# Issuing the first samples from SP and ACT, holding back weights and the second unit's samples, and reordering rows and copies at the start of a routed MLP kernel

## The reference

```
s0  = relu(x @ swi[0]) @ swo[0]            # shared unit, all samples
s1  = relu(x @ swi[1]) @ swo[1]
eo  = relu(x @ wi[label]) @ wo[label]      # the sample's own expert, 256 -> 1024 -> 256
gate_in = concat(eo[:, 0], s0[:, 0], s1[:, 0])          # row 0 of each sample only
w   = softmax(relu(gate_in @ g1) @ g2)                   # 3 numbers per sample
x   = x + eo * w[0] + s0 * w[1] + s1 * w[2]
x   = x + zX * lap_x(x) + zY * lap_y(x) + zR * x * (1 - x)   # second differences, reflected edges
```

## Time and profile before

| what | us |
|---|---|
| median of 3 runs | 1146.95 (1146.84 to 1147.79) |
| the profiled execution, its own time | 1147.54 |
| its span, first to last instruction | 1146.0 |
| PE busy | 1137.4 (99% of the span) |
| DVE busy | 676.5 (59%) |
| ACT busy | 455.7 (40%) |
| POOL busy | 79.8 (7%) |

### The profile page before, as it was taken

The page is one execution under the profiler, slowest core; times in us unless marked ns, Lnnn a source line. Parts: engine busy times, 40 slices in busy tenths (PEclk is TensorE's granted clock), DMA queues, the critical chain, the costliest instruction groups (busy, mean ns, idle before and its releaser), DMA issues.

```text
span 1146.0 us, 16857 instructions
## 1 busy us (share of the span) xinstructions
PE 1137.4 (99%) x6068; PEld 971.9 (85%) x6068; DVE 676.5 (59%) x1030; ACT 455.7 (40%) x808; POOL 79.8 (7%) x125
## 2 busy tenths in 40 slices
PE   8999999999999999999999999999999999999998
PEld 7888888888888888888888888888888888888888
DVE  4656666656666644556555655565465565556556
ACT  2555555555655532323323333333333233333323
POOL 3111211211211100000000000000000000000001
PEclk9999999999999999999999999999999999999999
DMA  8555556556565514023022121131230230321300
GB/s 277 158 162 170 171 169 204 180 152 195 179 191 150 163 34 117 16 68 78 17 73 46 47 76 27 57 84 23 62 83 16 69 81 13 74 45 49 75 29 24
DMA packets 111252, 111.83 MB, mean 98 GB/s; under 512 B 78441, under 2 KB 87234, under 8 KB 111170
## 3 DMA queue, kind: packets, MB, share of 16 engines
q1 hardware_dynamic: 96770, 59.71, 19.4%
q0 software_dynamic: 14016, 50.73, 14.8%
q10 hardware_dynamic: 384, 0.33, 0.1%
HBM read 89.40 MB, written 17.04 MB: 93 GB/s over the span
## 4 chain that ended last, share of the span: by engine, by line
PE 98%; DMA 1%; DVE 0%; issue 0%; ACTq 0%; ACT 0%; POOL 0%; DVEq 0%; POOLq 0%
PE acc L917 31%; PE hbank L890 16%; PE hbank L889 16%; PE hbank L891 16%; PE acc L918 16%; PE tbank L845 1%; DMA xs<-in_x 1%; PE acc L903 0%; PE hbank L870 0%; PE tbank L840 0%; PE acc L928 0%; PE acc L810 0%; PE acc L930 0%; PE acc L929 0%; PE tbank L853 0%
## 5 line engine op out<-in xcount | busy, mean ns | idle before, releaser
L582 DVE SCALAR_TENSOR_TENSOR hl<-hbank,hh 128x512 fp32r<-128x512 f32 (+2 forms) x440 | 275.7, 627 | 426.9 <-ACT hh L1022 426.3
L1022 ACT ACTIVATE hh<-hbank 128x512 fp32r<-128x512 f32 (+2 forms) x440 | 240.2, 546 | 587.9 <-PE hbank L891 584.9
L917 PE MATMUL acc<-swo,hh 128*128 128x512 f32 x992 | 359.3, 396 | 0.0
L918 PE MATMUL acc<-swo,hl 128*128 128x256 f32 x992 | 277.8, 280 | 0.0
L917 PEld LDWEIGHTS acc<-swo,hh 128*128 128x128 f32 x992 | 186.3, 188 | 43.7
L889 PE MATMUL hbank<-xh,swh 128*128 128x512 f32 (+1 forms) x528 | 205.3, 389 | 0.0
L890 PE MATMUL hbank<-xl,swh 128*128 128x512 f32 (+1 forms) x528 | 205.0, 388 | 0.0
L891 PE MATMUL hbank<-xh,swl 128*128 128x512 f32 (+1 forms) x528 | 202.1, 383 | 0.0
L917 PE MATMUL acc<-ewo,hh 128*128 128x512 f32 x528 | 194.6, 398 | 0.7 <-DVE rx L590 0.4
L918 PEld LDWEIGHTS acc<-swo,hl 128*128 128x128 f32 x992 | 187.1, 189 | 9.6
L918 PE MATMUL acc<-ewo,hl 128*128 128x256 f32 x528 | 148.0, 280 | 0.0
(11 more groups left out here) (194 smaller groups left out, 900.5 us busy)
## 6 DMA issues: line engine op xcount, KB each, us to landing
rw<-in_L_cond_wi POOLq DMA_DIRECT2D x44, 512.0 KB, 4.5
rw<-in_L_cond_wo POOLq DMA_DIRECT2D x44, 512.0 KB, 4.6
eo_scratch<-eo SPq DMA_DIRECT2D x128, 64.0 KB, 2.6
xs<-in_x SPq DMA_DIRECT2D x16, 512.0 KB, 4.3
rw<-in_x SPq DMA_DIRECT2D x256, 32.0 KB, 2.2
ei<-eo_scratch SPq DMA_DIRECT2D x16, 512.0 KB, 5.5
xs<-in_x SPq DMA_DIRECT2D x127, 64.0 KB, 3.5
out<-ot SPq DMA_DIRECT2D x15, 512.0 KB, 6.3
```

The lines of the kernel that those rows point to most:

```text
L582: e.scalar_tensor_tensor(h_slot(HL, g), bank[:, 0:w], 0.0, h_slot(HH, g).bitcast(F32), ALU.max, ALU.subtract).then_inc(h_lo, 1)
L917: e.matmul(acc[j][:, 0:2 * D], HH[:, g % NH, js], woc[:, c, :], start=(c == 0), stop=False)
L918: m = e.matmul(acc[j][:, D:2 * D], HL[:, g % NH, js], woc[:, c, 0:D], start=False, stop=last)
L1022: e.activation(h_slot(HH, g), hbank[g % HRING][:, 0:w], ACT.Relu).then_inc(h_hi, 1)
```

## The change

FIRST_BY gives samples 0 to 3 of unit 0 to ACT and 4 to 7 to SP; GpSimd loads none, and its semaphore `xp_in` goes. ACT issues at g == EARLY - 1 with EARLY = 6, so behind the relu of chunk 5, and the relus of chunks 6 and 7 are DVE's. GpSimd waits for `h_prod` 12 ahead of pieces 2, 1, 3 of unit 0, and SP waits for `h_prod` 12 ahead of unit 1's samples. The row of samples gets its own bank (`acc[2]`) and its own signal `row_prod`, so that DVE copies it behind one product of three; the float copy goes. PE puts the second products of chunks 2 and 3 ahead of the first products of chunks 4 and 5. Unit 0's transposes move from (2, 0) to (1, 7), still behind the first product of chunk 15 but now ahead of the second product of chunk 13, and unit 0's first product waits for each half of the low part by itself. DVE makes the low part of weight piece 0 at (1, 5) and not at (1, 7), and `evacuate(1)` stands ahead of `cut_low(2, 2)`.

```diff
@@ -28,10 +28,10 @@
-EARLY = 8
+EARLY = 6
 LAST_ORDER = (0, 2, 1, 3)
-FIRST_BY = {"ACT": (0, 1, 2), "SP": (3, 4, 5), "POOL": (6, 7)}
+FIRST_BY = {"ACT": (0, 1, 2, 3), "SP": (4, 5, 6, 7)}
@@ -81,7 +81,7 @@
-    if (n, c) == (2, 0):
+    if (n, c) == (1, 7):
         return [(1, 0), (1, 1)]
@@ -135,8 +135,8 @@
 SHARED_AT = (4, 6, 8, 10, 11, 13, 15, 17)
-FIRST_HIGH = {(1, 6): [(2, 0)], (2, 0): [(2, 2)], (2, 1): [(2, 1)], (2, 3): [(2, 3)]}
-FIRST_LOW = {(1, 7): [(2, 0)], (2, 0): [(2, 2)], (2, 2): [(2, 1)], (2, 4): [(2, 3)]}
+FIRST_HIGH = {(1, 4): [(2, 0)], (2, 0): [(2, 2)], (2, 1): [(2, 1)], (2, 3): [(2, 3)]}
+FIRST_LOW = {(1, 5): [(2, 0)], (2, 0): [(2, 2)], (2, 2): [(2, 1)], (2, 4): [(2, 3)]}
@@ -218,7 +218,7 @@
         msel = sb("msel", [128, NSLOT])
-        rowf = sb("rowf", [1, 2, NSLOT])
+        rowf = sb("rowf", [1, NSLOT])
         tab = sb("tab", [1, 3, NSLOT], I32)
@@ -264,6 +264,7 @@
         t_prod = sem("t_prod")
+        row_prod = sem("row_prod")
         t_hi = sem("t_hi")
@@ -271,7 +272,6 @@
         s_in = sem("s_in")
-        xp_in = sem("xp_in")
         w_hi = sem("w_hi")
@@ -380,8 +380,6 @@
             x_slot[tile % 2] += 16 * (slots_of(tile - 1)[1] if 1 <= tile <= NU else 1)
-            if tile == 1:
-                x_slot[1] -= 16 * len(FIRST_BY["POOL"])
             X_VAL[tile] = x_slot[tile % 2]
@@ -488,18 +486,17 @@
             def slot_table():
+                e.wait_ge(row_prod, 1)
+                e.tensor_copy(tab[:, 0, :], acc[2][0:1, 0:NSLOT]).then_inc(*V.up())
+                AT["samples"] = V.n
                 e.wait_ge(t_prod, T_AT["rows"])
-                e.tensor_copy(tab[:, 0, :], tbank[0:1, 0:NSLOT]).then_inc(*V.up())
-                AT["samples"] = V.n
-                e.tensor_copy(tab[:, 2, :], tbank[0:1, 2 * NSLOT:3 * NSLOT]).then_inc(*V.up())
+                e.tensor_copy(tab[:, 2, :], tbank[0:1, NSLOT:2 * NSLOT]).then_inc(*V.up())
                 AT["experts"] = V.n
-                e.tensor_copy(rowf[:].rearrange("p a n -> p (a n)"), tbank[0:1, 0:2 * NSLOT]).then_inc(t_free, 1)
+                e.wait_ge(consts, 7)
+                e.scalar_tensor_tensor(rowf[:], tbank[0:1, 0:NSLOT], 0.5, outdef[:],
+                                       ALU.is_lt, ALU.mult).then_inc(t_free, 1)
                 e.wait_ge(t_free, T_AT["rows"])
-                e.wait_ge(consts, 7)
-                e.scalar_tensor_tensor(rowf[:, 1, :], rowf[:, 1, :], 0.5, outdef[:],
-                                       ALU.is_lt, ALU.mult).then_inc(*V.up())
-                e.wait_ge(dve_seq, V.n)
-                e.tensor_tensor(tab[:, 1, :], rowf[:, 0, :], rowf[:, 1, :], ALU.add).then_inc(*V.up())
+                e.tensor_tensor(tab[:, 1, :], acc[2][0:1, 0:NSLOT], rowf[:], ALU.add).then_inc(*V.up())
                 AT["targets"] = V.n
@@ -715,6 +712,8 @@
                     slot_table()
+                if (n, c) == (1, NC - 1):
+                    hidden_low(g)
                 if g < G:
@@ -739,8 +738,9 @@
                 if (n, c) == (2, 0):
+                    evacuate(1)
                     cut_low(2, 2)
-                if g < G:
+                if g < G and (n, c) != (1, NC - 1):
                     hidden_low(g)
@@ -748,7 +748,7 @@
                     own_slot()
-                if g >= LAG and CHUNKS[g - LAG][1] == NC - 1 and CHUNKS[g - LAG][0] < NP - 2:
+                if g >= LAG and CHUNKS[g - LAG][1] == NC - 1 and CHUNKS[g - LAG][0] < NP - 2 and g - LAG != 2 * NC - 1:
                     evacuate(CHUNKS[g - LAG][0])
@@ -820,10 +820,9 @@
                 e.wait_ge(dve_seq, AT["msel"])
-                for a in range(2):
-                    e.matmul(tbank[0:1, a * NSLOT:(a + 1) * NSLOT], cols[:, a:a + 1], msel[:], start=True, stop=True)
-                e.matmul(tbank[0:1, 2 * NSLOT:3 * NSLOT], cols[:, 2:3], msel[:], start=True,
-                         stop=True).then_inc(t_prod, 1)
+                e.matmul(acc[2][0:1, 0:NSLOT], cols[:, 0:1], msel[:], start=True, stop=True).then_inc(row_prod, 1)
+                e.matmul(tbank[0:1, 0:NSLOT], cols[:, 1:2], msel[:], start=True, stop=True)
+                e.matmul(tbank[0:1, NSLOT:2 * NSLOT], cols[:, 2:3], msel[:], start=True, stop=True).then_inc(t_prod, 1)
@@ -831,7 +830,8 @@
                 if tile == 1:
-                    e.wait_ge(xp_in, 16 * len(FIRST_BY["POOL"]))
+                    e.wait_ge(dve_seq, AT["targets"])
                 if k is None:
@@ -874,7 +874,7 @@
                     to = bank[:, 0:w]
-                    if c == 0:
+                    if c == 0 and tile > 1:
                         e.wait_ge(t_free, T_AT[tile_last(tile)])
@@ -886,6 +886,8 @@
                 for k in range(2):
+                    if tile == 1 and c == 0:
+                        e.wait_ge(t_free, T_AT[tile, k])
                     e.matmul(to, wh[:, k, cs], xh[k], start=(k == 0), stop=False)
@@ -941,6 +943,8 @@
                     slot_rows()
+                if (n, c) == (1, NC - 1):
+                    first_product(g)
                 if g < G:
@@ -972,10 +976,14 @@
                     second_product(g - 1)
-                if g < G:
+                if g < G and (n, c) != (1, NC - 1):
                     first_product(g)
-                if g >= LAG and (n, c) not in ((2, 0), (2, 1)) and CHUNKS[g - LAG][0] < NP - 1:
+                if g >= LAG and (n, c) not in ((0, 4), (0, 5), (2, 0), (2, 1)) and CHUNKS[g - LAG][0] < NP - 1:
                     second_product(g - LAG)
+                if (n, c) == (0, 3):
+                    second_product(g - 1)
+                    second_product(g)
             for j, c in LAST_PRODUCTS:
@@ -1102,7 +1110,7 @@
                             cut_high(ws, p)
-                if (n, c) == (0, NC - 1):
+                if g == EARLY - 1:
                     first_samples()
@@ -1164,11 +1172,8 @@
             load_unit(0, (0,))
-            for b in FIRST_BY["POOL"]:
-                e.reg_load(reg, tab[0:1, 0, b:b + 1])
-                v = e.snap(reg, min_val=0, max_val=NS - 1)
-                e.dma_start(XS[1][b:128:8, :, :], x[bass.ds(v, 1), :, :].rearrange("a (p j) d -> (a p) j d", p=16)) \
-                    .then_inc(xp_in, 16)
+            e.wait_ge(h_prod, 12)
             load_unit(0, (2, 1, 3))
```

## The result

The changed kernel takes 1148.57 us, the median of 18 runs (1147.58 to 1150.47), against 1146.80 for the kernel before in its 18 (1145.17 to 1147.79). The ratio is 1.0017 with a 95% interval of 1.0010 to 1.0024. It is slower by 1.8 us, where I forecast no change at 1147.1 and a range that ended at 1148.2. The profiled execution took 1148.16 us, its span is 1146.6.

The account below looks back on a forecast made before the run. PE, busy 99% of the span, was taken as the bound. A 2.66 us gain on unit 0 would be spent waiting for unit 1's samples, net +0.1 us, so 1147.1 us, with a range of 1144.7 to 1148.2.

Parts of the forecast that it names:

- The wait for the gate-row copy: Ahead of unit 0's first second product: PE's 0.4 us wait for DVE goes, bringing the gain so far to 2.66 us.
- the one ahead of unit 0's first product: PE's 0.8 us wait there goes; the product starts at 24.55 in place of 26.54, 2.0 us gained.
- SP's first issue of unit 1: Behind the twelfth product (18.95): first sample issued at 19.4, eighth at 26.5, landing 6.4 us later at 32.9.
- The standstill in front of unit 1's transposes: PE wants these transposes at 30.2 but starts at 33.0, waiting for samples: idle for 2.8 us.
- the 2.66 us are gained and then spent: Ahead of unit 1's transposes: PE gains 2.66 us on unit 0, then loses it waiting for unit 1's samples.
- +0.1: Net effect at unit 1's transposes: they start at 33.0 against 32.9, so the time moves by +0.1 us.
- the third rival, "the clock falls, slower": Behind PE's idle stretch at unit 1's transposes, 5 us at the lower clock lose 2.5 us: 1149.6; chance 0.04.
- The first samples of unit 0: Ahead of unit 0's transposes: the last sample lands before 22.3, so they start at 22.35 without wait, 1.5 us earlier.

Follow-up runs that it names:

- the filled kernel: Changed kernel with ten extra matmuls, results overwritten, on PE ahead of its wait for unit 1's samples: 1147.11 us, ratio 1.0006.
- the second group: The changed kernel timed again, unaltered, beside other follow-up kernels: 1149.28 us, ratio 1.0021 against the kernel before.
- half the filling: Changed kernel with five extra matmuls instead of ten on PE ahead of its wait for unit 1's samples: 1148.12 us, ratio 1.0012.

## Why the prediction was wrong

**What held.** PE's idle time was what the edits moved, though not all that was at stake. The wait for the gate-row copy and the one ahead of unit 0's first product went, as costed: 2.13 us from unit 0's transposes to its first product against 2.2 forecast, and 4.27 from there to the second product against 4.2. SP's first issue of unit 1 came 0.5 us behind the twelfth product, as forecast, the eighth 7.37 us behind that against 7.11, and landing took 6.8 against 6.4. The standstill in front of unit 1's transposes was forecast at 2.8 us and is 2.55 and 2.96 in the two profiled executions. That is close partly by luck: the eighth issue was 0.3 us and its landing 0.4 us later than forecast, while the rest of the list was sooner, as the clock had risen earlier than in the kernel before. The step "the 2.66 us are gained and then spent" is what the filled kernel shows by itself: 0.5 us over the kernel before, not told from +0.1 by its interval.

**What failed.** The step that failed is the third rival, "the clock falls, slower", which I gave 0.04 and left out of the range. It comes in 17 of 18 executions and in 9 of 11 of the second group. Its price was 2.5 us, for 5 us at the lower level; measured are 3.4 us at that level and 1.6 us lost between two marks of the trace. The forecast's +0.1 for the late samples and the trace's +1.6 for the clock make +1.7, against +1.8 measured (+2.7 in the second group of runs, where 1.0 us stays unexplained). By the filled kernel the parts are 0.5 us and 1.5 to 2.2 us. I argued against it from the one standstill the trace had, 1.0 us, which had left the clock alone. A row for 1.0 us says nothing about 2.8 us, nearly three times as long, so the case had no evidence against it and deserved far more than 0.04 and a place in the range. The Trainium skill, "TensorE: Matmul & The Clock Gate", Part 1, says that idleness returns the array to its lower level, and here the trace agrees, with 0.54 granted from 32.5 to 35.9 behind 2.55 us of standing still.

**A smaller miss.** The first samples of unit 0 were to land before PE asked. In the profiled execution the last was issued at 15.33 and took 6.0 us (DMA view below), and PE stood 0.8 us (in the other profiled execution it didn't stand); with the clock high early, PE comes sooner than the kernel before showed. It is the same trap: an execution with another start of the clock has other margins. That wait most likely cost nothing here, as the next one was longer. The Trainium skill, "DMA: Bandwidth & Descriptors", "Anatomy of one DMA", has about 2.0 us fixed and the bytes over 436 GB/s, fitted to GpSimd's own DMAs, which makes an estimate of 2.15 us for 64 KB. This trace has 3.8 to 7.3 for the samples that SP and ACT issue, and the measurement decides.

```profile
xs<-in_x SPq DMA_DIRECT2D x1, 64.0 KB, 6.0
```

**What stays open.** Which standstill lets the clock fall isn't settled. In the profiled executions it fell behind 2.34, 2.55 and 2.96 us and did not behind 2.69 and 3.02 us ahead of unit 0's transposes, and with half the filling it fell in 5 of 11 executions of one kernel. With none of the filling it fell in 26 of 29, with all of it in none of 11. So length raises the odds but doesn't decide alone. The two that kept the clock stand at another place in PE's list, and no run here put the same standstill at both places.

## What to carry to other kernels

When several transfers are issued one by one from one queue, the last one's issue time sets the date, here twelve at 1.0 us each and 6.5 us to land. Removing PE's waits ahead of it only moves the standing still. The four kernels without SP's wait show it: with all twelve issues on SP they take 1146.38 us with GpSimd's wait and 1146.42 without (the kernel before: 1146.62). With four of them on ACT it is 1144.89 with GpSimd's wait and 1146.89 without. The gain needed both. Where a forecast moves small waits into one long one, price the slower clock behind it and give it a real chance. It cost 1.6 us here, nearly the whole result.

## What was not expected of the hardware

Ten matmuls that compute nothing made the kernel faster by 1.5 to 2.2 us, by keeping PE from standing still. What they save is the lower clock behind the standstill. And the moment at which the clock first rises differs between executions of one program (ahead of the first gate-row product at 5.7 us in one profiled execution of the changed kernel, near 9.5 in the other), which shifts the start of the table, the samples and the weights. The executions of the kernel before lie 2.6 us apart from lowest to highest; this may be part of it, but how much wasn't measured.
